# One-hot tables of the routing laid with token blocks innermost and compared in bf16

## The reference

```python
xn = layernorm(x)                                   # 2048 tokens x 256
q, k, v = xn @ Wq + bq, xn @ Wk + bk, xn @ Wv + bv  # 16 heads of 16
y = softmax(causal(q @ k.T / 4)) @ v @ Wo + bo
top2_logits, top2 = top_k(xn @ Wr, 2)               # of 8 experts
w = softmax(top2_logits)
ffn = sum over the token's 2 experts of w[e] * ((clip(silu(xn @ Wg[e]), -7, 7) * (xn @ Wu[e])) @ Wd[e])
out = x + y + ffn
```

## Time and profile before

| | |
|---|---|
| time, median of 3 runs | 438.12 us (437.99 to 438.84) |
| the profiled execution's own time | 438.36 us |
| its span | 436.4 us |
| TensorE (PE) busy | 412.3 us, 94% |
| VectorE (DVE) busy | 332.0 us, 76% |
| ScalarE (ACT) busy | 222.4 us, 51% |
| GpSimd (POOL) busy | 196.5 us, 45% |

### The profile page before, as it was taken

One profiled execution on the slowest core, in us unless ns is written; L12 is line 12 of the kernel. 1 busy time (PEld: TensorE's weight loads), 2 busy tenths in 40 slices (PEclk: granted clock), 3 DMA queues, 4 the chain that ended last, 5 costly groups with the idle time before them and its releaser, 6 DMA issues.

```text
span 436.4 us, 8151 instructions
## 1 busy us (share of the span) xinstructions
PE 412.3 (94%) x2755; PEld 246.4 (56%) x2755; DVE 332.0 (76%) x1043; ACT 222.4 (51%) x511; POOL 196.5 (45%) x223
## 2 busy tenths in 40 slices
PE   8998979989999999999799999999999999999993
PEld 8585414655364465566547567565667476556332
DVE  6827999999989859775287866789396988881795
ACT  1563362334646566545164355456555445646970
POOL 5331266576064187256474265415655255313320
PEclk9999979999999999999899999999999999999996
DMA  7289896788067089235954239805595336110782
GB/s 228 82 218 194 289 200 211 226 285 282 3 160 174 1 252 279 75 110 170 214 168 156 103 110 249 248 24 182 164 235 178 136 101 194 24 26 6 236 271 72
DMA packets 40372, 71.33 MB, mean 163 GB/s; under 512 B 5893, under 2 KB 30598, under 8 KB 40332
## 3 DMA queue, kind: packets, MB, share of 16 engines
q0 software_dynamic: 9360, 39.99, 29.1%
q1 hardware_dynamic: 27132, 26.76, 25.0%
q10 hardware_dynamic: 3840, 4.08, 3.7%
HBM read 55.85 MB, written 15.60 MB: 164 GB/s over the span
## 4 chain that ended last, share of the span: by engine, by line
PE 68%; DVE 21%; DMA 4%; issue 4%; ACT 1%; POOL 1%; SPq 0%; ACTq 0%; DVEq 0%; POOLq 0%
PE psum L1293 14%; PE psum L1330 14%; PE psum L1254 11%; PE psum L1273 11%; PE psum L1339 8%; DVE psum L981 7%; DVE mxa L984 4%; PE psum L1209 3%; PE psum L1185 3%; PE psum L1312 3%; DMA bqk<-in_bqk 2%; PE psum L1320 2%; DMA xg<-xn_rows,token 2%; DVE resid L953 1%; DMA x<-in_x 1%
## 5 line engine op out<-in xcount | busy, mean ns | idle before, releaser
L894 ACT ACTIVATE probs<-psum 128x512 f32<-128x512 f32 (+1 forms) x320 | 151.1, 581 | 40.9 <-PE psum L1273 40.3
L981 DVE CUSTOM_DVE_ANT_0 psum<-psum,maskrow 128x128 f32<-128x128 f32 (+3 forms) x256 | 121.4, 506 | 14.3 <-PE psum L1254 14.0
L1254 PE MATMUL psum<-packk,packq 96*128 96x512 bf16 (+3 forms) x384 | 94.2, 328 | 3.3 <-DVE mxb L981 1.2
L1273 PE MATMUL psum<-packq,packk 99*128 99x512 bf16 (+3 forms) x384 | 91.0, 330 | 3.3 <-ACT probs L894 2.1
L984 DVE TENSOR_REDUCE mxa<-psum 128x1 f32<-128x512 f32 x128 | 87.7, 685 | 5.4 <-PE psum L1254 5.3
L1293 PE MATMUL psum<-probs,v 128*32 128x512 f32 (+3 forms) x768 | 75.7, 503 | 1.0 <-POOL probs L821 0.9
L1254 PEld LDWEIGHTS psum<-packk,packq 96*128 96x128 bf16 x384 | 35.1, 97 | 56.1 <-issue 15.9
L821 POOL TENSOR_SCALAR_AFFINE_SELECT probs<-probs 128x512 f32<-128x512 f32 (+1 forms) x48 | 41.2, 863 | 44.8 <-ACT probs L894 44.7
L1273 PEld LDWEIGHTS psum<-packq,packk 99*128 99x128 bf16 x384 | 33.4, 98 | 42.7 <-issue 10.5
L788 POOL DMA_INDIRECT xg<-xn_rows,token x39 | 37.7, 967 | 38.9 <-PE psum L1320 27.4
L806 POOL DMA_INDIRECT expert_rows<-wvr,slots x39 | 39.3, 1008 | 31.8 <-ACT wvr L914 17.2
(11 more groups left out here) (120 smaller groups left out, 457.8 us busy)
## 6 DMA issues: line engine op xcount, KB each, us to landing
qk_parts<-stage SPq DMA_DIRECT2D x24, 256.0 KB, 3.9
stage<-expert_rows SPq DMA_DIRECT2D x16, 256.0 KB, 4.1
packq<-qk_parts SPq DMA_DIRECT2D x16, 192.0 KB, 5.4
packk<-qk_parts SPq DMA_DIRECT2D x14, 192.0 KB, 5.8
x<-in_x SPq DMA_DIRECT2D x4, 512.0 KB, 6.2
packq<-qk_parts SPq DMA_DIRECT2D x16, 128.0 KB, 6.0
xn_rows<-probs ACTq DMA_DIRECT2D x4, 512.0 KB, 14.7
out<-x SPq DMA_DIRECT2D x16, 128.0 KB, 3.0
```

Of the source, the lines that this page charges most:

```text
L894: act.activation(probs[:, g % RING, h, 0:width], psum[:, bank, 0:width], ACT.Exp, scale=SCALE)\
L981: ins = dve.tensor_tensor_reduce(out=chunk, in0=chunk, in1=maskrow[:, BANK - width:], scale=1.0, scalar=NEG, op0=ALU.add, op1=ALU.max, acc ...
L1254: pe.matmul(psum[:, bank, 0:width], packq[0:MAXROW, u % SLOTS, i // HALF, h, P * (i % HALF):P * (i % HALF + 1)], packk[0:MAXROW, u % SLOTS ...
L1273: ins = pe.matmul(psum[:, bank, at:at + width], packk[0:KROWS, u % SLOTS, j // HALF, h, P * (j % HALF):P * (j % HALF + 1)], packq[0:KROWS, ...
```

## The change

The two tables get the block number t as innermost index: `row_hot` is [k, row, t] instead of [k, t, row], `digits` is [k, digit, tile, t] instead of [k, t, digit, tile]. The row and tile numbers are cast to bf16 (`row_of`, `tile_of`, two new instructions at the end of `place_slots`), and the counters that they are compared with, so far one row of 128 (`iota_row`, bf16) and one of 39 (`iota_t`, float32) that the instruction repeated, are written in full size in bf16 (`iota_rows`, 2048 values, `iota_tiles`, 624) by a fourth stage of constants on GpSimd. `high_digit` becomes bf16. TensorE reads each table of the list product in steps of 16 values. The planner is told new durations and the new stage.

```diff
-    for n, (ns, due) in enumerate(((1100, -30), (2000, 30), (1800, 31))):
+    for n, (ns, due) in enumerate(((1100, -30), (2000, 30), (1800, 31), (4500, 15000))):
         job("POOL", ("const", n), ns, due=due)
...
-    dve(("place",), 3700, [("PE", ("route",))], 20003, frees=("route",))
+    dve(("place",), 4000, [("PE", ("route",))], 20003, frees=("route",))
     for k in range(2):
-        dve(("rows", k), 2300, [("DVE", ("place",))], 20004)
-        dve(("tiles", k), 2950, [("DVE", ("place",))], 20004)
+        dve(("rows", k), 1250, [("DVE", ("place",)), ("POOL", ("const", 3))], 20004)
+        dve(("tiles", k), 1300, [("DVE", ("place",)), ("POOL", ("const", 3))], 20004)
...
+            def counters_beside_tokens():
+                pool.iota(iota_rows[:, :, :], pattern=[[1, P], [0, NT]], base=0, channel_multiplier=0,
+                          allow_small_or_imprecise_dtypes=True)
+                chain(pool.iota(iota_tiles[:, :, :], pattern=[[1, MAX_TILES], [0, NT]], base=0, channel_multiplier=0,
+                                allow_small_or_imprecise_dtypes=True))
...
+                dve.tensor_copy(row_of[:, :, :], posrow[:, :, :])
+                dve.tensor_copy(tile_of[:, :, :], postile[:, :, :]).then_inc(pos_ready, 1)
...
-                dve.tensor_tensor(row_hot[:, k, :, :], iota_row[:, :].unsqueeze(1).to_broadcast([P, NT, P]),
-                                   posrow[:, k, :].unsqueeze(2).to_broadcast([P, NT, P]), ALU.is_equal).then_inc(rows_ready, 1)
+                dve.tensor_tensor(row_hot[:, k, :, :], iota_rows[:, :, :],
+                                  row_of[:, k, :].unsqueeze(1).to_broadcast([P, P, NT]), ALU.is_equal).then_inc(rows_ready, 1)
...
-                low, high = digits[:, k, :, 0, :], digits[:, k, :, 1, :]
-                shape = [P, NT, MAX_TILES]
-                chain(route_step, dve.tensor_tensor(low, iota_t[:, :].unsqueeze(1).to_broadcast(shape),
-                                                    postile[:, k, :].unsqueeze(2).to_broadcast(shape), ALU.is_equal))
-                dve.tensor_tensor(high, low, high_digit[:, :].unsqueeze(2).to_broadcast(shape), ALU.mult)
+                low, high = digits[:, k, 0, :, :], digits[:, k, 1, :, :]
+                shape = [P, MAX_TILES, NT]
+                chain(route_step, dve.tensor_tensor(low, iota_tiles[:, :, :], tile_of[:, k, :].unsqueeze(1).to_broadcast(shape), ALU.is_equal))
+                dve.tensor_tensor(high, low, high_digit[:, :].unsqueeze(1).to_broadcast(shape), ALU.mult)
                 dve.tensor_scalar(low, low, low_digit[:, k:k + 1], None, ALU.mult).then_inc(digits_ready, 1)
...
-                    ins = pe.matmul(psum[:, bank, 0:2 * MAX_TILES], row_hot[:, k, t, :],
-                                    digits[:, k, t, :, :].rearrange("p n j -> p (n j)"), start=n == 0, stop=n == 2 * NT - 1)
+                    ins = pe.matmul(psum[:, bank, 0:2 * MAX_TILES], row_hot[:, k, :, t],
+                                    digits[:, k, :, :, t].rearrange("p n j -> p (n j)"), start=n == 0, stop=n == 2 * NT - 1)
```

More of the change, by code:

```diff
@@ L516, in build @@
         iota_t = sb("iota_t", [P, MAX_TILES])
-        iota_row = sb("iota_row", [P, P], BF16)
         low_digit = sb("low_digit", [P, 2])
-        high_digit = sb("high_digit", [P, NT])
+        high_digit = sb("high_digit", [P, NT], BF16)
         lg = sb("lg", [P, NT, E])
@@ L539, in build @@
         posrow = sb("posrow", [P, 2, NT], I32)
+        tile_of = sb("tile_of", [P, 2, NT], BF16)
+        row_of = sb("row_of", [P, 2, NT], BF16)
         below = sb("below", [P, MAX_TILES, E])
@@ L559, in build @@
         z = stage[:, :, :, :].rearrange("p a b t -> p (a b t)").bitcast(F32).rearrange("p (r k d) -> p r k d", k=2, d=D)
-        row_hot = yt[:, :, :].rearrange("p c t -> p (c t)").bitcast(BF16).rearrange("p (k t r) -> p k t r", k=2, r=P)
-        digits = wexp_own[:, :, :].rearrange("p s w -> p (s w)").bitcast(BF16)[:, 0:2 * NT * 2 * MAX_TILES]\
-            .rearrange("p (k t n j) -> p k t n j", k=2, t=NT, n=2)
+        row_hot = yt[:, :, :].rearrange("p c t -> p (c t)").bitcast(BF16).rearrange("p (k r t) -> p k r t", k=2, t=NT)
+        free_weights = wexp_own[:, :, :].rearrange("p s w -> p (s w)").bitcast(BF16)
+        homes = [2 * 2 * MAX_TILES * NT, P * NT, MAX_TILES * NT]
+        digits = free_weights[:, 0:homes[0]].rearrange("p (k n j t) -> p k n j t", k=2, n=2, t=NT)
+        iota_rows = free_weights[:, homes[0]:sum(homes[:2])].rearrange("p (r t) -> p r t", t=NT)
+        iota_tiles = free_weights[:, sum(homes[:2]):sum(homes)].rearrange("p (j t) -> p j t", t=NT)
         psum = ctx.enter_context(nc.psum_tensor("psum", [P, BANKS, BANK], F32))
@@ L754, in counters @@
                 for to, pattern, base, step in ((iota8, [[1, E]], 0, 0), (iota128, [[P, NT]], 0, 0),
-                                                (iota_t, [[1, MAX_TILES]], 0, 0), (iota_row, [[1, P]], 0, 0),
+                                                (iota_t, [[1, MAX_TILES]], 0, 0),
                                                 (low_digit, [[1, 2]], 0, 2), (high_digit, [[1, NT]], 1, 0)):
@@ L759, in counters @@
                 chain(ins)
+            def counters_beside_tokens():
[3 more added lines that the diff above has]
+                                allow_small_or_imprecise_dtypes=True))
             def constants(n):
-                (identities, mask_and_ones, counters)[n]()
+                (identities, mask_and_ones, counters, counters_beside_tokens)[n]()
                 pool.sem_inc(consts, 1)
```

6 lines of the change are left out of this document (5 added, 1 removed).

## The result

The changed kernel took 440.22 us (median of 20 runs, 437.90 to 442.56), the kernel before beside it 438.06 us (20 runs). The ratio is 1.0041, 95% interval 1.0022 to 1.0060: slower by about 1.8 us. The profiled execution has a span of 439.6 us against 436.4, a difference of 3.2. It is more than the 1.8 mostly because the profiled execution of the changed kernel (441.55 us) lies 1.3 us above its median and that of the kernel before (438.36) only 0.3.

The account below looks back on a forecast made before the run. VectorE was taken to bound 36 to 111 us, TensorE 111 to 200. That VectorE stretch starts 6.5 us later and holds 5.7 less, +0.8 on 438.36: 439.2 us, against a median forecast of 438.9, range 435.2 to 442.5.

Parts of the forecast that it names:

- case (a): Whole kernel: late start and VectorE's saving nearly cancel, 437.0 to 440.5 us; chance 0.40.
- The late start, +6.5: TensorE's first row-maxima product 6.5 us later: q/k waiting for normalisation +4.3, lower clock +1.3, changed order +0.9.
- VectorE's saving, −5.7: VectorE's table block before the list product: 10.7 us falls to 4.7, two new casts add 0.3, net 5.7 less.
- The wide comparison: VectorE's 2048-value row-table comparison, all bf16: 1.22 us instead of 2.28, 1.14 each with overlap.
- the step of the 624-value instructions: VectorE's digit-table instructions: 0.48 us each by formula; with waits and overlaps 0.50, 0.40 and 0.30.
- The counters, 2.3 us and hidden: GpSimd writes two counters before the first reciprocal deviation: 2.3 us, at most 6.5, hidden even then.
- The list product, costed at nothing: TensorE's list product reading tables in 32-byte steps: nothing added to its 1.72 us; VectorE has 2.6 us other work.
- rival (e): Strided reads triple the list product to 5.2 us, VectorE waits 2.6 us, time 441.5 us; chance 0.13.
- The order behind 111 us, costed at nothing: TensorE's rewritten order after 111 us: zero in the mean, though a stall could shift it 3 us either way.
- (b): 36 to 111 us: TensorE cannot follow, only half the saving is paid, 441.8 us; chance 0.17.
- (c): 36 to 111 us and start: granted clock stays 1.0, giving 435.6 us; chance 0.26.
- (d): VectorE's comparison stays at 1.04 ns a value, saving missing, 444.6 us; chance 0.04.

Follow-up runs that it names:

- start_only: Kernel before with only the fourth stage of constants (4500 ns) added to its plan, counters written but unused, old tables: 444.85 us, ratio 1.0161.
- plan_all: Changed kernel, planner told measured costs (list product 5.0 us, digits 1.9 us), counters booked behind GpSimd's fourth q/k residual: 433.13 us, ratio 0.9900 to the kernel before.
- warm: Changed kernel with 96 warm-up products on TensorE instead of 60: 439.66 us, ratio 1.0034 to the kernel before.
- rows_only: As idle, but the digit table (moving operand) keeps its old layout and comparison: 437.63 us, ratio 0.9988 to the kernel before.
- four: As idle, but only four token blocks innermost, steps of 8 bytes in both operands: 438.04 us in its one run.
- frozen: Changed tables in the kernel before's engine order, counters written by GpSimd behind the second deviation: 442.86 us, ratio 1.0107 to the kernel before.
- idle: As frozen, but GpSimd writes the counters behind its fourth q/k residual: 442.14 us, ratio 1.0100 to the kernel before.
- later: Changed kernel with the counters planned behind the second deviation (3400 ns), planner free to order the rest: 442.39 us, ratio 1.0095 to the kernel before.
- eight: As idle, but only eight token blocks innermost, steps of 16 bytes in both operands: 441.29 us, ratio 1.0075 to the kernel before.
- digits_only: As idle, but the row table (stationary operand) keeps its old layout and comparison: 442.77 us, ratio 1.0095 to the kernel before.

## Why the prediction was right or wrong

The prediction was 438.9 us with 437.0 to 440.5 for its likeliest case (a), start and saving nearly cancel. 440.22 lies in both ranges, 1.3 us above the number. The terms show that the nearness is in part luck:

**The late start, +6.5: right for this execution.** Measured +7.2 in the timeline of TensorE. It hangs on when the loads land: start_only, with the same order at the start, has +4.3 at the same landmark, because VectorE waited for neither of the last two chunks. That the time of start_only rose by 6.8 is therefore no second measurement of the 6.5. The change against plan_all, which has the old start, is 7.5 us of the same landmark (43.08 against 35.58), though these two orders differ in more. Its parts: q/k at 19.97 against 19.5 with the clock counted in, the clock's part 1.0 to 1.7 (warm) against 1.3. Chunk 3 arrived about as read from the loads: its statistics start at 13.08, against 12.5.

**VectorE's saving, −5.7: too large.** The block with its casts fell from 10.7 to 6.4 us: 4.3. The wide comparison was right (1.22 predicted, 1.21 and 1.23 measured). The Trainium skill, "VectorE: DVE Perf Modes", section "The perf-mode tier table", lists 1224 ns for a two-input operation on 2048 bf16 values, and the trace agrees. What failed is the step of the 624-value instructions: predicted 0.50, 0.40, 0.30 in sequence, measured 0.48 and 0.91 for the comparison, 0.80 and 1.26 for the first product. The slow product instances lie beside GpSimd's masks; GpSimd's timeline of the change:

```profile
64.75 0.70 POOL L831 TENSOR_SCALAR_AFFINE_SELECT probs<-probs 128x512 f32<-128x512 f32 x1 [5.60 <-ACT probs L904]
66.28 2.72 POOL L831 TENSOR_SCALAR_AFFINE_SELECT probs<-probs 128x512 f32<-128x512 f32 x2 [0.83 <-ACT probs L904]
```

The comparison shows it too. VectorE's rows of plan_all, then GpSimd's:

```profile
55.24 1.43 DVE L1130 TENSOR_TENSOR wexp<-wexp,tile_of 128x624 bf16<-128x624 bf16 x1
56.71 0.48 DVE L1131 TENSOR_TENSOR wexp<-wexp,high_digit 128x624 bf16<-128x624 bf16 x1
...
58.53 0.92 DVE L1130 TENSOR_TENSOR wexp<-wexp,tile_of 128x624 bf16<-128x624 bf16 x1
59.49 0.48 DVE L1131 TENSOR_TENSOR wexp<-wexp,high_digit 128x624 bf16<-128x624 bf16 x1
```

```profile
54.92 1.42 POOL L786 TENSOR_TENSOR stage<-resid,stage 128x512 bf16<-128x512 f32 x1 [3.52 <-ACT stage L884]
58.14 0.99 POOL L833 TENSOR_SCALAR_AFFINE_SELECT probs<-probs 128x512 f32<-128x512 f32 x1 [1.80 <-ACT probs L906]
```

Each slow instance of 624 values overlaps an instruction of GpSimd that was already running, and ends 0.32 to 0.33 us after it: 56.67 after 56.34, 59.45 after 59.13, and in the change 65.78 after 65.45. Those that overlap none take the 0.48 us of the formula, and so does one that had started before the mask (64.47 in the change, mask from 64.75). The wide comparison was not slowed (1.21 us at 66.01), but it too had started first; in rows_only it is a mask that starts 0.08 us after a wide comparison which is slow, 1.65 us against 0.99 in four. In these rows whichever engine starts second waits. No run took GpSimd's work away from there, so this is a reading of the traces.

**The counters, 2.3 us and hidden: half right.** They take 3.3 us (2.48 and 0.83), within the bound of 6.5, and nothing waits for them. That they slow VectorE beside them was not in the working: frozen and idle show it, 5.40 against 2.83 us for eight tiles, and in the change the small instruction `vareps` of chunk 0 took 2.10 us instead of 0.17, up to the end of the first counter.

**The list product, costed at nothing: wrong.** This is the step that failed: the prediction added no time for reads in steps of 32 bytes and no wait of VectorE behind them. What came is rival (e): it put 5.2 us on a product that took 4.93, and 2.6 us on VectorE's wait, which was 2.06. Of the growth from 1.72 at most 0.35 us is the lower clock, since a contiguous product at 0.50 took 2.07 (start_only). The prediction weighed the rival at 0.13 because no row showed the stride's price. No run has the change's order with a contiguous product, so what the wait of 2.06 us is worth in the change's time is a sum and not a measurement.

**The order behind 111 us, costed at nothing: wrong by about 3.3 us.** The gather stall of before is gone; the prediction had named such a stall as 3 us either way and left it out of the sum. Summed on the span: `slot_pad` 6.5 us later (start 7.2, block −4.3, wait 2.1, and 1.5 of other order between), less the stall 3.3, gives the measured 3.2. Against the forecast that is +0.7 for the start, +1.4 for the block, +2.1 for the wait, +1.5 and −3.3 for the order: the number came out near because the last term took back most of the others, and that was luck.

**The other rivals.** (b) wants under 3 us of idle TensorE between the first row maxima and 105 us; it stood 7.85 us there, so it was not that it could not follow. (c) wants a granted clock of 1.0 from 36 to 111 us; it was 0.89. (d) fell with the comparison's 1.21 us.

What the tables are worth by themselves is shown only in the order of before, where they change the time by +0.2 us with a product of 2.5 us (four, in its one run) and by +4.3 with one of 5.0 (idle). From start_only to the change it is −4.6 us and from before to plan_all −4.7, but in both pairs the order changes too; in the first, a gather stall of 3.7 us goes away. Why later, with nearly the start of plan_all and `slot_pad` only 1.05 us behind it, has a span 7.8 us longer stays open beyond three pieces: VectorE's wait (1.87 against 0.21), TensorE's busy time from 36 to 111 us (63.4 us against 68.1), and its clock in that stretch (0.91 against 0.93). No run separates what in the order does it.

## What to carry to other kernels

When a layout is turned to please one engine, price the reader too, and probe its stride before costing it at nothing: here the writer gained 4.3 us and the product, by its moving operand, lost 3.2. A saving is worth what the next engine can take up: with TensorE behind exponentials and value products, 4 us on VectorE became a wait of 7 us. Where a planner writes the order, feed it the measured costs on both sides of the edit: with 2600 ns booked for a product of 4.9 us and the counters ahead of the first deviation the same tables came out 0.4% slower; with costs near the measured ones, and the new order that these gave, 1.0% faster.

## What the runs showed of the hardware

**A strided moving operand.** The same 32 products of 128x78 took 1.72 us contiguous (before, through a rise of the granted clock; 2.07 at 0.50 in start_only), 2.54 in steps of 8 bytes (four), 4.85 in steps of 16 (eight) and 4.98 in steps of 32 (idle): 54, 79, 152 and 156 ns each. In the last three both operands are strided; the moving one alone, in steps of 32 bytes, takes 4.73 (digits_only). The rule weighed in the prediction (the Trainium skill, "SBUF — State Buffer", section "Door 1: The DMA port swizzle") has bf16 free up to 8 elements, 16 bytes. The measurement differs and decides: 8 elements are as dear as 16, and 4 already cost half again. That 16 and 32 bytes cost the same fits the 16-byte lines of the same paragraph: in both, each value lies in another line. For weight loads the step matters less: alone, in rows_only, it takes a load from 117 ns to 174 and the product to 2.21 us.

**The pace of the strided product does not follow the clock.** In frozen the product runs through a rise of the granted clock; windows of TensorE's work there:

```profile
66.00:68.00 2.00, 2.00 (x16) 1.77 (x13) 0.00 (x0) 0.00 (x0) 0.00 (x0) 0.63 0.33 53
68.00:70.00 2.00, 2.00 (x16) 1.96 (x15) 0.00 (x0) 0.00 (x0) 0.00 (x0) 1.00 0.00 0
```

It takes 4.98 us so, and 4.93 in the change at 0.50 throughout (1.00 is 2.4 GHz, 0.50 is 1.2). The strided reads bound it, not the array.

**Strided writes of VectorE** in bf16, 32 bytes apart, took 4.3 ns a value (8.81 us for 2048) against 1.1. **GpSimd beside VectorE**: writing counters nearly doubled float32 normalisations of 256 values (0.35 to 0.68 us each).
